# Four-layer graph network on one core: no drains between VectorE's one-hot steps, and the row chain of the first layer dealt out anew

## The chip, the core and the metric

One core of a Trainium2 chip runs the whole program in one launch. The metric is the device time of that launch in microseconds; of a kernel several runs are shown, and their median is compared. A page of the profile and a trace come from one further, profiled execution.

## What is computed

6250 nodes of 128 features, 206,250 directed edges sorted by destination. Each of four layers normalizes the rows, applies relu, sums messages over the edges and adds a result to the residual stream. The change touches the first layer alone:

```python
h = jnp.maximum(_layernorm(x, axis=-1), 0.0)
msg = edge_val[:, None] * h[edge_src]
neighbor = segment_sum(msg, edge_dst, num_segments=6250)
out = neighbor @ W1.T + b1 + (h * neighbor) @ W2.T + b2
x = x + leaky_relu(out, negative_slope=0.2)
h = jnp.maximum(_layernorm(x, axis=-1), 0.0)      # rows for layer 2
```

Layers 2 to 4 (two aggregations over the same edges, a graph norm, a gated update) reuse a table of edge counts that the first layer's stage leaves in DRAM.

## The kernel before

**Sorting and tables** (to about 130 us): edges are laid into groups; four tables (key, source low part, high and low part of the edge weight) end up in `carry`.

**The counting stage** (about 130 to 1190 us) is where the change lies. The nodes are cut into 49 blocks of 128; a *half* h handles the edges into block h. A half has 8 *duos* (`DUOS`), a duo has 2 *supergroups* (16 per half, `SGS`). The engines split the work, each in its own hand-written order, joined by semaphores:

- **VectorE** (`half_onehots`, L1691) makes the one-hot tiles of a duo in a ring of four slots (`RING`). `make_onehots` waits until TensorE has used the slot (`weight_ready`), then writes source and cell one-hots (L1634, L1635). `weigh_onehots` multiplies the cell one-hots by the two weight parts (L1639, L1640) and raises `onehots`. In step j it makes duo j and weighs duo j-1, so that no instruction follows directly on one it depends on; then come pieces of the *row chain* of older blocks, and a `dve.drain()` (L1721) closes the step.
- **TensorE** (`half`, L833) takes a duo when `onehots` says so: per supergroup 4 matmuls for counts (L800) and 8 for weights (L806) into PSUM. After every fourth supergroup comes a part of `weigh` (L817): 24 or 26 float32 instructions that multiply last half's weights with the normalized rows, so that a whole weighted sum of one block takes 98 of them. A transpose (`row_T`, L826) and two matmuls (`lin1`, L830, L831) of the row chain stand between.
- **ScalarE** (`take_half`, L1195) copies counts (L1176) and weights (L1182) of each supergroup out of PSUM; TensorE may be two supergroups ahead in counts and four in weights. It also scales the block's sum (`take_sum`, L1193, in the first supergroup of a half) and takes the square root of the row chain (`row_std`, L1186).
- **SyncE** (`half`, L494) stores the counts, loads and stores rows.

**The row chain** of block g: `prod1` (sum times h), `lin1`, `add_bias1`, `leaky`, `add_x`, `row_stats`, `row_mean`, `row_var`, the square root on ScalarE, `row_rstd`, `row_norm`, `row_relu` (two instructions), `row_rest`. Before, it is spread over the steps of halves g+2 (`prod1` in step 6), g+3 (steps 0 to 5, and 7) and g+4 (steps 0 to 2).

Halves 0 to 4 are written out as straight code on VectorE; from half 5 on two halves make one turn of a loop (`dve.Fori`), in which addresses and semaphore values come from registers. After the loop the rest of the row chain of the last blocks runs alone (the *tail*), then the edge counts are read back for the next layer (L887, L917).

```python
for j in range(DUOS):
    make_onehots(h * DUOS + j, j % RING)
    if not (first and j == 0):
        weigh_onehots(h * DUOS + j - 1, (j - 1) % RING)
    ...
    dve.drain()
```

Of the kernel before, what the change touches and what calls it, by code (L numbers as in the profile page):

```python
# [42 lines left out]
RING = 4  # L43
# [38 lines left out]
def build_gnn(nc, A, out):  # L82
    with ExitStack() as ctx:
# [264 lines left out]
        def _(sp):  # L348
# [141 lines left out]
            def count_sorted():  # L490
# [94 lines left out]
            branch(sp, order, edges_any(3), load_pieces(3))  # L585
# [140 lines left out]
        def _(pe):  # L726
# [381 lines left out]
        def _(act):  # L1108
# [86 lines left out]
            def take_half(h, par, i, summed=True, normed=True):  # L1195
                for s in range(SGS):
# [3 lines left out]
                    if s == 9 and normed:  # L1200
                        row_std(h - 3)

            def count_sorted():
# [8 lines left out]
                with act.Fori(1, NHALF // 2) as i:  # L1212
                    take_half(i * 2 + 1, 1, i)
                    take_half(i * 2 + 2, 0, i + 1)
                take_sum(NB - 2, 1)
                row_std(NB - 3)
# [143 lines left out]
        def _(dve):  # L1360
# [330 lines left out]
            def half_onehots(h, par, summed=True, last=True, oldest=True, first=False):  # L1691

                for j in range(DUOS):
                    make_onehots(h * DUOS + j, j % RING)
                    if not (first and j == 0):
                        weigh_onehots(h * DUOS + j - 1, (j - 1) % RING)
                    if oldest:
                        if j == 0:
                            row_norm(par)
                        if j == 1:  # L1700
                            row_relu(h - 4, par)
                        if j == 2:
                            row_rest(h - 4, par)
                    if last:
                        if j == 0:
                            add_bias1(h - 3)
                        if j == 1:
                            leaky()
                        if j == 2:
                            add_x(h - 3, 1 - par)  # L1710
                        if j == 3:
                            row_stats(1 - par)
                        if j == 4:
                            row_mean()
                        if j == 5:
                            row_var()
                        if j == 7:
                            row_rstd(h - 3)
# [17 lines left out]
            def row_planes(g, par):  # L1736
# [5 lines left out]

            def row_end(g, par):
                row_rstd(g)
                dve.drain()
                row_planes(g, par)
# [16 lines left out]
            def count_sorted():  # L1763
# [3 lines left out]
                half_onehots(0, 0, False, False, False, True)  # L1767
                half_onehots(1, 1, False, False, False)
                half_onehots(2, 0, True, False, False)
                half_onehots(3, 1, True, True, False)  # L1770
                half_onehots(4, 0)
                with dve.Fori(2, NHALF // 2) as i:
                    half_onehots(i * 2 + 1, 1)
                    half_onehots(i * 2 + 2, 0)
                weigh_onehots(NDUO - 1, RING - 1)

                dve.drain()
                for j in range(3):
# [4 lines left out]
                row_planes(NB - 4, 1)  # L1783
                row_sum(NB - 3, 0)
                prod1(NB - 2, 1)
                row_end(NB - 3, 0)
                row_sum(NB - 2, 1)
                prod1(NB - 1, 0)
                row_end(NB - 2, 1)
                row_sum(NB - 1, 0)  # L1790
# [257 lines left out]
```

## Time and profile before

| | |
|---|---|
| median of 3 runs | 2363.23 us (2360.51 to 2366.76) |
| profiled execution | 2367.89 us, its span 2366.2 us |
| PE / PEld / DVE / ACT busy | 2041.8 / 1810.6 / 1538.2 / 1229.5 us |
| counting stage: PE, DVE, ACT busy of 1036.40 us (154.40 to 1190.80) | 1009.72, 904.39, 631.35 us |
| largest groups | L1176 398.6, L817 577.0, L806 417.9, L1182 407.8, L1634 271.5, L1639, L1640, L1635 219.5 us each |

Busy times are unions of an engine's instructions; matmuls are pipelined, so a busy PE isn't PE at its peak. An instruction's duration reaches past the start of the next one where the two overlap, so a step is measured from start to start. A wait on "issue" is idle time for which the trace shows no instruction that ended it.

### The profile page before, as it was taken

How to read it: one execution, taken by the hardware profiler on the slowest of the kernel's cores; microseconds unless marked ns; L12 is line 12 of the kernel's file. 1: busy time of each engine (PE TensorE's matmuls, PEld its weight loads, DVE VectorE, ACT ScalarE, POOL GpSimd, SP SyncE). 2: the span in 40 equal slices, each digit the busy share in tenths (PEclk: the TensorE clock that was granted, in tenths of full speed). 3: DMA queues.
4: the chain of work that ended last, by engine and by line, in shares of the span. 5: the costliest groups of instructions: out<-in, count | busy, mean ns of one | idle time of the engine just before them, and what ended most of it. 6: DMA issues, size and time to landing. Idle time of an engine off the chain costs nothing.

```text
span 2366.2 us, 63380 instructions
## 1 busy us (share of the span) xinstructions
PE 2041.8 (86%) x22497; PEld 1810.6 (77%) x22542; DVE 1538.2 (65%) x3147; ACT 1229.5 (52%) x3115; POOL 136.3 (6%) x120
## 2 busy tenths in 40 slices
PE   1269999999999999999989999999986239999897
PEld 1169999999999999999976666668886238888444
DVE  8588888888888888888855565657855850000133
ACT  4856666666666666666636676678865200000232
POOL 5500000000000000000000000000002410000000
PEclk7579999999999999999999999999998569999898
DMA  8312222122212222221243333325841459888121
GB/s 242 105 60 78 81 95 95 64 94 95 88 69 95 95 74 84 95 95 63 95 158 119 117 117 117 107 107 192 322 148 51 118 197 334 301 300 271 40 69 39
DMA packets 184330, 300.84 MB, mean 127 GB/s; under 512 B 12626, under 2 KB 135943, under 8 KB 184159
## 3 DMA queue, kind: packets, MB, share of 16 engines
q1 hardware_dynamic: 180364, 287.55, 35.0%
q0 software_dynamic: 3904, 12.50, 1.8%
q8 instruction: 35, 0.57, 0.1%
q14 instruction: 27, 0.22, 0.0%
HBM read 199.52 MB, written 100.48 MB: 127 GB/s over the span
## 4 chain that ended last, share of the span: by engine, by line
PE 40%; DVE 28%; DVEq 15%; issue 10%; ACT 2%; DMA 2%; POOL 1%; ACTq 1%; POOLq 0%; SPq 0%; PEldq 0%
PE ps L917 22%; DVEq L1721 8%; DVE edge_area L1640 7%; DVE edge_area L1635 5%; PE ps L901 5%; DVE edge_area L1639 4%; PE ps L887 3%; PE ps L1038 3%; PE ps L817 3%; DVE edge_area L1634 1%; PE ps L957 1%; DVE hT_s L1488 1%; DVEq L1634 1%; POOL edge_area L643 1%; PE ps L806 1%
## 5 line engine op out<-in xcount | busy, mean ns | idle before, releaser
L1176 ACT CAST edge_area<-ps 128x392 f16<-128x392 f32 x784 | 398.6, 508 | 422.0 <-PE ps L800 421.6
L817 PE MATMUL ps<-big,rows_area 128*128 128x128 f32 x4802 | 577.0, 277 | 0.3 <-ACT agg_s L1193 0.3
L817 PEld LDWEIGHTS ps<-big,rows_area 128*128 128x128 f32 x4802 | 551.8, 192 | 0.6 <-ACT agg_s L1193 0.6
L806 PE MATMUL ps<-edge_area 128*128 128x98 f16 x6272 | 417.9, 208 | 0.0
L1182 ACT COPY big<-ps 128x392 f32<-128x392 f32 x784 | 407.8, 520 | 1.1 <-PE ps L806 0.7
L1634 DVE TENSOR_TENSOR edge_area<-lo_pair,carry 128x1024 f16<-128x1024 f16 x392 | 271.5, 693 | 130.5 <-issue 102.8
L806 PEld LDWEIGHTS ps<-edge_area 128*128 128x128 f16 x6272 | 332.6, 98 | 0.0
L800 PE MATMUL ps<-edge_area 128*128 128x98 f16 x3136 | 276.5, 209 | 38.8 <-DVE edge_area L1640 35.5
L917 PE MATMUL ps<-big,agg 128*128 128x256 f16 (+1 forms) x2450 | 290.1, 278 | 0.0
L917 PE MATMUL ps<-big,rows_area 128*128 128x256 f16 (+1 forms) x2450 | 264.3, 272 | 25.6 <-DMA big<-edge_counts 25.6
L917 PEld LDWEIGHTS ps<-big,rows_area 128*128 128x128 f16 x2450 | 236.6, 98 | 53.5 <-DMA big<-edge_counts 25.9
L917 PEld LDWEIGHTS ps<-big,agg 128*128 128x128 f16 x2450 | 239.0, 101 | 30.6
L1248 ACT ACTIVATE edge_area<-ps,edge_area 128x896 bf16<-128x896 f32 x182 | 173.5, 1004 | 128.7 <-DVE edge_area L1822 75.4
L800 PEld LDWEIGHTS ps<-edge_area 128*128 128x128 f16 x3136 | 189.2, 98 | 61.9 <-issue 39.3
L1639 DVE TENSOR_TENSOR edge_area<-edge_area,carry 128x784 f16<-128x784 f16 x392 | 219.5, 560 | 0.2 <-issue 0.2
L1640 DVE TENSOR_TENSOR edge_area<-edge_area,carry 128x784 f16<-128x784 f16 x392 | 219.5, 560 | 0.0
L1635 DVE TENSOR_TENSOR edge_area<-cell_pair,carry 128x784 f16<-128x784 f16 x392 | 219.4, 560 | 0.0
L1266 ACT ACTIVATE edge_area<-big 128x256 f16<-128x256 f16 (+1 forms) x525 | 209.4, 404 | 15.4 <-DMA big<-edge_counts 8.2
L1843 DVE TENSOR_REDUCE out_part<-big 128x4 f32<-128x1024 f16 (+1 forms) x175 | 202.1, 1189 | 0.0
L1835 DVE TENSOR_TENSOR carry<-carry,ps 128x896 f32<-128x896 f32 x85 | 92.3, 1086 | 143.0 <-PE ps L901 143.0
L1863 DVE TENSOR_SCALAR agg<-ps 128x256 f32 (+2 forms) x25 | 10.5, 419 | 258.4 <-PE ps L917 258.4
L1327 ACT COPY hT_s<-ps 128x896 f32<-128x896 f32 x7 | 6.3, 906 | 297.2 <-PE ps L948 297.2
(235 smaller groups left out, 1854.1 us busy)
## 6 DMA issues: line engine op xcount, KB each, us to landing
big<-edge_counts SPq DMA_DIRECT2D x336, 448.0 KB, 4.6
edge_counts<-edge_area SPq DMA_DIRECT2D x49, 1568.0 KB, 5.6
hs<-node_rows POOLq DMA_DIRECT2D x14, 448.0 KB, 4.1
edge_area<-x_stream SPq DMA_DIRECT2D x14, 448.0 KB, 3.9
node_rows<-rows_area SPq DMA_DIRECT2D x1, 3136.0 KB, 13.1
agg_s<-node_rows SPq DMA_DIRECT2D x49, 64.0 KB, 4.9
agg_s<-in_x SPq DMA_DIRECT2D x49, 64.0 KB, 4.4
x_stream<-agg_s SPq DMA_DIRECT2D x49, 64.0 KB, 2.5
```

The source lines that it names most:

```text
L800: last = mm(pair_of(p_count[s % 2], c), sources_of(slot, r, c), cells_of(oh_cell, slot, r, c), start=(c == 0), stop=(c == 3), skip_group_c ...
L806: last = mm(pair_of(p_weight[s % 4], c), sources_of(slot, r, c), cells_of(oh, slot, r, c), start=(c == 0 and oh is oh_whi), stop=(c == 3 a ...
L817: last = mm(p_sum, h0[:, n, :], w32[:, par, n, :], start=(n == 0), stop=(n == NB - 1))
L917: last = mm(p_block[par][:, 0:width, :], planes1[:, sh, p, :] if l == 1 else planes[:, p, sh, :], piece[:, par, k, 0:width, j, :], start=( ...
L1176: nc.scalar.copy(store_slot[:, par, :, cols], p_count[s % 2]).then_inc(sem("count_taken"), 1)
L1182: nc.scalar.copy(w32[:, par, :, cols], p_weight[s % 4]).then_inc(sem("weight_taken"), 1)
L1266: last = nc.scalar.activation(unused[:, j, 0:width, :], piece[:, par, k, 0:width, j, :], ACT.Copy, accum_out=out_part[:, par, sh:sh + 1])
L1634: V.tensor_tensor(oh_src[:, slot], paired(lo_pair, P), lo.to_broadcast([P, 4, P, 2]), ALU.is_equal)
L1635: V.tensor_tensor(oh_cell[:, slot], paired(cell_pair, CELLS), key.to_broadcast([P, 4, CELLS, 2]), ALU.is_equal)
L1639: V.tensor_tensor(oh_whi[:, slot], oh_cell[:, slot], whi.to_broadcast([P, 4, CELLS, 2]), ALU.mult)
L1640: V.tensor_tensor(oh_wlo[:, slot], oh_cell[:, slot], wlo.to_broadcast([P, 4, CELLS, 2]), ALU.mult).then_inc(sem("onehots"), 1)
L1843: V.tensor_reduce(out_part[:, par, k * SHS:k * SHS + KD], piece[:, par, k, 0:width, 0:KD, :].rearrange("p q n d -> p n q d"), AX_XY, ALU.a ...
```

## The change

1. VectorE's steps lose their `dve.drain()`. In its place each step waits, after it has issued the one-hots of duo d, until `onehots` shows that the weights of duo d-2 are done; then the row chain's instructions follow, and `weigh_onehots` of duo d-1 closes the step (it stood right behind `make_onehots`). The very first step keeps a drain and raises `onehots` by one, and TensorE's wait goes up by one to match.
2. The row chain of block g is dealt out anew: `prod1` in step 7 of half g+2; `add_bias1`, `leaky`, `add_x`, `row_stats` in steps 4, 5, 6, 7 of half g+3; `row_mean`, `row_var` in steps 0, 1 and `row_rstd`, `row_norm`, `row_relu` in steps 5, 6, 7 of half g+4; `row_rest` in step 0 of half g+5. It ends one half later.
3. TensorE's `row_T` moves from supergroup 3 to 7, `lin1` from 11 to 15; ScalarE's square root from supergroup 9 to 3, for a block one older. SyncE stores an x row before it loads the next one.
4. In the tail, which holds one block's chain more, the instructions of two blocks alternate, with drains.

```diff
@@ SyncE
                 def half(h, b, par, older=True):
                     load_h_row(h - 1, 1 - par)
+                    store_x(h - 3, 1 - par)
                     load_x_row(h - 2, par)
-                    store_x(h - 3, 1 - par)
...
                 load_h_row(NB - 1, 0)
+                store_x(NB - 3, 0)
                 load_x_row(NB - 2, 1)
-                store_x(NB - 3, 0)
                 store_h(NB - 4, 1)
+                store_x(NB - 2, 1)
                 load_x_row(NB - 1, 0)
-                store_x(NB - 2, 1)
                 store_h(NB - 3, 0)
@@ TensorE
-                    pe.wait_ge(sem("onehots"), h * DUOS + s // 2 + 1)
+                    pe.wait_ge(sem("onehots"), h * DUOS + s // 2 + 2)
...
-                        if rows and s == 3:
+                        if rows and s == 7:
                             row_T(h - 2, par)
...
-                        if rows and s == 11:
+                        if rows and s == SGS - 1:
                             lin1(h - 2, par)
@@ ScalarE
-                    if s == 9 and normed:
-                        row_std(h - 3)
+                    if s == 3 and normed:
+                        row_std(h - 4)
@@ VectorE
                 for j in range(DUOS):
                     make_onehots(h * DUOS + j, j % RING)
-                    if not (first and j == 0):
-                        weigh_onehots(h * DUOS + j - 1, (j - 1) % RING)
+                    if first and j == 0:
+                        dve.drain()
+                        dve.sem_inc(sem("onehots"), 1)
+                        continue
+
+                    dve.wait_ge(sem("onehots"), h * DUOS + j)
+                    if written and j == 0:
+                        row_rest(h - 5, 1 - par)
                     if oldest:
                         if j == 0:
+                            dve.sem_inc(sem("passed"), 1)
+                            row_mean()
+                        if j == 1:
+                            row_var()
+                        if j == 5:
+                            row_rstd(h - 4)
+                        if j == 6:
                             row_norm(par)
-                        if j == 1:
+                        if j == 7:
                             row_relu(h - 4, par)
...
-                    if summed and j == 6:
+                    if summed and j == 7:
                         prod1(h - 2, par)
-                    dve.drain()
+                    weigh_onehots(h * DUOS + j - 1, (j - 1) % RING)
```

How the instructions stand on VectorE in the loop, the step that holds `row_var` (`TENSOR_SCALAR rstd<-mv`); ISA rows are register work, drains are not listed. Before:

```order
L1632 ISA
L1634 ISA [waits weight_ready]
L1634 TENSOR_TENSOR edge_area<-lo_pair,carry 128x1024
L1635 ISA
L1635 TENSOR_TENSOR edge_area<-cell_pair,carry 128x784
L1639 ISA
L1639 TENSOR_TENSOR edge_area<-edge_area,carry 128x784
L1640 ISA
L1640 TENSOR_TENSOR edge_area<-edge_area,carry 128x784
L1667 TENSOR_SCALAR rstd<-mv 128x1
```

The same step of the change (its lines are numbered six higher):

```order
L1638 ISA
L1640 ISA [waits weight_ready]
L1640 TENSOR_TENSOR edge_area<-lo_pair,carry 128x1024
L1641 ISA
L1641 TENSOR_TENSOR edge_area<-cell_pair,carry 128x784
L1673 TENSOR_SCALAR rstd<-mv 128x1 [waits onehots]
L1645 ISA
L1645 TENSOR_TENSOR edge_area<-edge_area,carry 128x784
L1646 ISA
L1646 TENSOR_TENSOR edge_area<-edge_area,carry 128x784
```

The row instruction now stands between making and weighing, and carries the wait on `onehots`; the number of instructions is the same.

The last step of a half in the change, VectorE, with the most row instructions of all steps:

```order
L1687 ISA [waits onehots]
L1688 TENSOR_SCALAR hT_s<-hT_s 128x128 [waits h1_out]
L1690 ISA
L1690 TENSOR_SCALAR agg<-hT_s 128x128
L1667 BN_STATS stats<-agg_s 128x6
L1650 REGISTER_ALU
L1653 TENSOR_TENSOR agg_s<-ps,agg_s 128x128 [waits hT1,sum_taken]
L1645 ISA
L1645 TENSOR_TENSOR edge_area<-edge_area,carry 128x784
```

Before, these four instructions stood in steps 1, 3 and 6; now all are ahead of the weighing of duo 6, and the last of them waits for TensorE's transpose (`hT1`).

## Rows read from the trace of the kernel before

**Rows 1.** The page, part 4: the chain that ended last, by engine and line.
```profile
PE 40%; DVE 28%; DVEq 15%; issue 10%; ACT 2%; DMA 2%; POOL 1%; ACTq 1%; POOLq 0%; SPq 0%; PEldq 0%
PE ps L917 22%; DVEq L1721 8%; DVE edge_area L1640 7%; DVE edge_area L1635 5%; PE ps L901 5%; DVE edge_area L1639 4%; PE ps L887 3%; PE ps L1038 3%; PE ps L817 3%; DVE edge_area L1634 1%; PE ps L957 1%; DVE hT_s L1488 1%; DVEq L1634 1%; POOL edge_area L643 1%; PE ps L806 1%
```
**Rows 2.** Waits, 130 to 1190 us: who waited for whom, us, times, longest.
```profile
DVE edge_area L1634 <- issue: 102.8, 284, 3.3
PE ps L800 <- DVE edge_area L1640: 35.5, 71, 7.1
```
**Rows 3.** Timeline, ScalarE, the copy of a block's sum: start, duration.
```profile
194.62 0.38 ACT L1193 ACTIVATE agg_s<-ps,w_unit 128x128 f32<-128x128 f32 x1
215.69 0.38 ACT L1193 ACTIVATE agg_s<-ps,w_unit 128x128 f32<-128x128 f32 x1
...
605.50 0.38 ACT L1193 ACTIVATE agg_s<-ps,w_unit 128x128 f32<-128x128 f32 x1
...
1170.31 0.38 ACT L1193 ACTIVATE agg_s<-ps,w_unit 128x128 f32<-128x128 f32 x1
```
**Rows 4.** Timeline, VectorE, straight code, a step without row instructions.
```profile
155.51 0.69 DVE L1634 TENSOR_TENSOR edge_area<-lo_pair,carry 128x1024 f16<-128x1024 f16 x1
156.12 0.56 DVE L1635 TENSOR_TENSOR edge_area<-cell_pair,carry 128x784 f16<-128x784 f16 x1
...
157.08 0.56 DVE L1640 TENSOR_TENSOR edge_area<-edge_area,carry 128x784 f16<-128x784 f16 x1
157.73 0.69 DVE L1634 TENSOR_TENSOR edge_area<-lo_pair,carry 128x1024 f16<-128x1024 f16 x1
```
**Rows 5.** Timeline, VectorE, straight code, end of the step with `row_var`.
```profile
221.42 0.56 DVE L1640 TENSOR_TENSOR edge_area<-edge_area,carry 128x784 f16<-128x784 f16 x1
221.90 0.15 DVE L1667 TENSOR_SCALAR rstd<-mv 128x1 f32<-128x1 f32 x1
222.14 0.69 DVE L1634 TENSOR_TENSOR edge_area<-lo_pair,carry 128x1024 f16<-128x1024 f16 x1
```
**Rows 6.** Timeline, VectorE, in the loop, end of the same step.
```profile
613.04 0.56 DVE L1640 TENSOR_TENSOR edge_area<-edge_area,carry 128x784 f16<-128x784 f16 x1
613.52 0.15 DVE L1667 TENSOR_SCALAR rstd<-mv 128x1 f32<-128x1 f32 x1
613.99 0.69 DVE L1634 TENSOR_TENSOR edge_area<-lo_pair,carry 128x1024 f16<-128x1024 f16 x1 [0.32 <-issue]
```
**Rows 7.** Windows: two halves at the loop's start, and one half in its middle.
```profile
217.10:259.20 42.10, 41.85 (x592) 41.16 (x590) 36.62 (x86) 26.27 (x69) 0.00 (x0) 1.00 0.25 89
600.10:621.96 21.86, 21.49 (x306) 20.94 (x303) 18.95 (x45) 13.59 (x36) 0.00 (x0) 1.00 0.24 85
```
**Rows 8.** Timeline, VectorE, in the loop, two row instructions in a row.
```profile
605.53 0.28 DVE L1688 SCALAR_TENSOR_TENSOR agg<-hT_s,agg 128x128 f32 x1
605.73 0.28 DVE L1658 TENSOR_TENSOR agg_s<-agg_s,hT_s 128x128 f32<-128x128 f32 x1
```
**Rows 9.** The chain in order of time, half 3: start, us, what.
```profile
194.88 0.51 ACT edge_area L1176
195.43 0.35 PE ps L800 x4
...
196.29 2.68 PE ps L817 x24
```
**Rows 10.** The chain in order of time, where it passes from VectorE to TensorE.
```profile
153.27 0.36 PE ps L800 x4
```
**Rows 11.** Timeline, the tail of the stage and the start of the next.
```profile
1202.92 0.37 ACT L1193 ACTIVATE agg_s<-ps,w_unit 128x128 f32<-128x128 f32 x1 [11.65 <-PE ps L817]
...
1204.37 4.28 PE L867 MATMUL ps<-carry,pick_row 128*25 128x128 f16 x75
...
1214.15 1.65 PE L887 MATMUL ps<-ident,big 128*128 128x128 f16 x14 [5.50 <-issue]
```
**Rows 12.** Timeline, VectorE, a wait for ScalarE's square root.
```profile
227.06 0.16 DVE L1671 RECIPROCAL rstd<-rstd 128x1 f32<-128x1 f32 x1 [0.38 <-ACT rstd L1186]
```

More of the change, by code:

```diff
@@ L584, in _, with summed_any @@
             stage(2, x_dram)
-            branch(sp, order, edges_any(3), load_pieces(3))
+            def summed_any():
+                sp.wait_ge(sem("agg_done"), 3)
+            branch(sp, order, both(edges_any(3), summed_any), load_pieces(3))
             sp.dma_start(hs[:], rows_of(rows_dram, 0)).then_inc(sem("h_in4"), 16)
@@ L1211, in count_sorted @@
                 take_half(2, 0, 1, True, False)
-                with act.Fori(1, NHALF // 2) as i:
+                take_half(3, 1, 1, True, False)
+                take_half(4, 0, 2)
+                with act.Fori(2, NHALF // 2) as i:
                     take_half(i * 2 + 1, 1, i)
@@ L1215, in count_sorted @@
                 take_sum(NB - 2, 1)
+                row_std(NB - 4)
                 row_std(NB - 3)
@@ L1689, in row_rest, with half_onehots @@
                                        op1=ALU.subtract).then_inc(sem("planes_ready1"), 1)
-            def half_onehots(h, par, summed=True, last=True, oldest=True, first=False):
+            def half_onehots(h, par, first=False, summed=True, last=True, oldest=True, written=True):
                 for j in range(DUOS):
                     make_onehots(h * DUOS + j, j % RING)
-                    if not (first and j == 0):
-                        weigh_onehots(h * DUOS + j - 1, (j - 1) % RING)
+                    if first and j == 0:
[5 more added lines that the diff above has]
+                        row_rest(h - 5, 1 - par)
@@ L1697, in half_onehots @@
                     if oldest:
                         if j == 0:
+                            dve.sem_inc(sem("passed"), 1)
[5 more added lines that the diff above has]
+                        if j == 6:
                             row_norm(par)
-                        if j == 1:
+                        if j == 7:
                             row_relu(h - 4, par)
-                        if j == 2:
-                            row_rest(h - 4, par)
@@ L1704, in half_onehots @@
                     if last:
-                        if j == 0:
+                        if j == 4:
                             add_bias1(h - 3)
-                        if j == 1:
+                        if j == 5:
                             leaky()
-                        if j == 2:
+                        if j == 6:
                             add_x(h - 3, 1 - par)
-                        if j == 3:
+                        if j == 7:
                             row_stats(1 - par)
-                        if j == 4:
-                            row_mean()
@@ L1715, in half_onehots @@
[L1715 to L1718, printed above, removed]
-                    if summed and j == 6:
+                    if summed and j == 7:
                         prod1(h - 2, par)
-                    dve.drain()
+                    weigh_onehots(h * DUOS + j - 1, (j - 1) % RING)
             def row_sum(g, par):
@@ L1734, in row_sum, with row_end @@
                 row_var()
-            def row_planes(g, par):
+            def row_end(g, par):
+                row_rstd(g)
+                dve.drain()
                 row_norm(par)
@@ L1741, in row_planes @@
                 row_rest(g, par)
[L1743 to L1746, printed above, removed]
             def rows_any():
@@ L1766, in count_sorted @@
                 dve.sem_inc(sem("mix_added"), 1)
[L1767 to L1771, printed above, removed]
+                half_onehots(0, 0, True, False, False, False, False)
+                half_onehots(1, 1, False, False, False, False, False)
+                half_onehots(2, 0, False, True, False, False, False)
+                half_onehots(3, 1, False, True, True, False, False)
+                half_onehots(4, 0, False, True, True, True, False)
                 with dve.Fori(2, NHALF // 2) as i:
@@ L1774, in count_sorted @@
                     half_onehots(i * 2 + 2, 0)
+                dve.drain()
                 weigh_onehots(NDUO - 1, RING - 1)
+                row_rest(NB - 5, 0)
+                add_bias1(NB - 3)
+                row_mean()
                 dve.drain()
+                leaky()
+                row_var()
                 for j in range(3):
@@ L1782, in count_sorted @@
                 V.memset(pick_row[:, DEG_BLOCKS - 1:DEG_BLOCKS], 1.0).then_inc(sem("bad_known"), 1)
-                row_planes(NB - 4, 1)
-                row_sum(NB - 3, 0)
-                prod1(NB - 2, 1)
-                row_end(NB - 3, 0)
-                row_sum(NB - 2, 1)
-                prod1(NB - 1, 0)
-                row_end(NB - 2, 1)
-                row_sum(NB - 1, 0)
+                add_x(NB - 3, 0)
+                row_rstd(NB - 4)
+                dve.drain()
+                row_stats(0)
+                row_norm(1)
+                dve.drain()
+                prod1(NB - 2, 1)
+                row_relu(NB - 4, 1)
+                row_mean()
+                dve.drain()
+                row_var()
+                row_rest(NB - 4, 1)
+                add_bias1(NB - 2)
+                dve.drain()
+                leaky()
+                row_rstd(NB - 3)
+                dve.drain()
+                add_x(NB - 2, 1)
+                row_norm(0)
+                dve.drain()
+                row_stats(1)
+                row_relu(NB - 3, 0)
+                dve.drain()
+                row_mean()
+                row_rest(NB - 3, 0)
+                dve.drain()
+                row_var()
+                prod1(NB - 1, 0)
+                dve.drain()
+                row_rstd(NB - 2)
+                add_bias1(NB - 1)
+                dve.drain()
+                leaky()
+                row_norm(1)
+                dve.drain()
+                add_x(NB - 1, 0)
+                row_relu(NB - 2, 1)
+                dve.drain()
+                row_stats(0)
+                row_rest(NB - 2, 1)
+                dve.drain()
+                row_mean()
+                dve.drain()
+                row_var()
                 row_end(NB - 1, 0)
```

## The prediction

> **What bounds the kernel now.** I read the chain that ended last first, because busy shares alone mislead here: the table has TensorE at 97% of the counting stage, yet the chain gives VectorE 28% of the span and VectorE's queue (DVEq) another 15%, and the one line L1721, the drain of `half_onehots`, has 8% by itself [rows 1]. 43% of a span of 2366.2 us is about 1017 us, which is nearly the counting stage: VectorE sets its pace. The waits say how: VectorE stood idle 284 times before L1634, the first instruction of a step, for 102.8 us in all with nothing but "issue" behind it, and TensorE waited 71 times for L1640 [rows 2].
>
> Next, the pace. ScalarE copies a block's sum once per half, always at the same place, so the distance of two copies is a half's period. It is 21.07 us from 194.62 to 215.69; from 215.69 to 1170.31 there are 44 halves in 954.62 us, 21.70 us each [rows 3]. The reader is to see that the same work runs at two paces. The early pace belongs to halves that VectorE had prepared in straight code, the late one to the loop. At the fast pace the chain runs through ScalarE's copy and TensorE [rows 9], and TensorE is busy 41.85 of 42.10 us [rows 7]: that is TensorE's own limit, with the same row chain in it. The difference, 0.63 us per half, is what VectorE costs today, and all that can be had from relieving it.
>
> **The cost of a drain.** Four one-hot instructions start 0.61, 0.48, 0.48 and, if nothing were between, 0.48 us apart: 2.05 us. Behind L1640 the next step starts 0.65 us later instead of 0.48 [rows 4], so in straight code a drain costs 0.17 us. With one short row instruction in the step, the next step follows 0.24 us after that instruction in straight code [rows 5] but 0.47 us in the loop [rows 6]. In the loop the register rows that compute addresses stand ahead of L1634, and behind a drain they can't be done while VectorE works. Between L1634 and L1640 there are register rows in the loop too, and the one-hots there start no farther apart than in straight code. So without the drain I expect both parts to go, the flush and the register work.
>
> **VectorE's need without drains.** One half in the loop has 45 instructions, 18.95 us busy of 21.86 [rows 7]. The busy time counts the last 0.08 us of L1640 (0.56 less 0.48), which overlaps with a successor once there is no drain: 8 of these take it to 18.3 us. Counted the other way: 8 steps of 2.05 are 16.4 us; 13 row instructions of some 0.15 to 0.34 us follow each other closer than they last, 0.20 for one of 0.28 [rows 8], some 1.9 us; together 18.3 us. TensorE's pace is 21.07. VectorE is left with 2.7 us per half, a third of a microsecond per step, before it sets the pace again.
>
> **What takes its place.** Each step now waits for `onehots` of duo d-2. Those weights were issued before the two one-hots of duo d: L1640 ends 0.08 us after its successor would start, and the instruction that carries the wait stands 1.09 us behind that start (0.61 and 0.48). I cost the new wait at nothing; the cover is the pair of one-hots. Its bounds: nothing, and at most what the drain cost.
>
> **The moved row chain.** No instruction is added in a half; on TensorE one transpose and four lin1 instructions move to other gaps of the same kind, so its pace stays. Who waits for whom: `prod1` in step 7 waits for the transpose behind supergroup 7; step 7 can only begin when TensorE has left duo 3, which is supergroup 7, so the transpose is finished while the one-hots of step 7 are made. `add_bias1` in step 4 needs `lin1` of the half before, and step 4 begins only when TensorE is through duo 0 of the next half, which is behind that lin1. `row_rstd` in step 5 needs ScalarE's root, which now stands behind the copies of supergroup 3, the very one that releases step 5: a wait like the 0.38 us of [rows 12] is likely every half. It is covered by the 2.7 us; without that cover it would cost 0.4 us times 45 halves, 17 us. Behind it in VectorE's queue is the weighing of duo 4, which TensorE needs only after it has worked through two duos and one part of `weigh` (2.7 us, [rows 9]). SyncE's queue: the store of x now waits for step 6 and h for step 7 instead of 2 and 1, and the counts of the half are stored behind them; both steps lie before TensorE ends the half, so nothing is late.
>
> **The sum**, against the profiled execution (2367.89 us):
> - The loop. 954.62 us less 44 times 21.07 (927.08) is 27.5 us; the 45th half, up to the tail, gives another 0.6. Minus 28.1 us.
> - The start. Until 153.27 us TensorE waits for VectorE duo by duo, without `weigh` [rows 10]: nine steps, 0.17 us each. Minus 1.5 us.
> - The tail. From the last sum copy on it is a chain of single instructions, and the next stage begins 5.50 us after TensorE's last count matmul with "issue" behind it [rows 11], which doesn't change. The last block's chain starts sooner behind `lin1`, but its instructions share their steps with another block's: three more of 0.2 to 0.3 us against 0.5 saved. The x row of the last block is loaded later, perhaps just late. Plus 0.3 us, between minus 1 and plus 3.
>
> Together minus 29.3 us: 2338.6 us for that execution. The median of the runs shown is 4.66 us below it, so 2333.9 us.
>
> **A rule that speaks against it.** The rows say that L1640 starts 0.48 us after an instruction that lasts 0.56, and 0.65 us after it where a drain stands between [rows 4]: the explicit drain costs something that instructions without one do not pay. The Trainium skill ("VectorE: DVE Perf Modes", section "The DRAIN you can't avoid") says that the pipe is flushed after every VectorE instruction whatever one does, that chaining copies without semaphores saved nothing, and that one should count instructions, not waits. By that rule the time would stay at 2363. The trace disagrees as far as it goes.
>
> **Rivals.**
> *No gain: the wait costs what the drain did.* If the wait for `onehots` keeps VectorE from preparing what follows, each step still loses the 0.42 us it loses today ((21.70 less 18.35) by 8), and the time stays at 2363. For it: the wait is a true dependency on VectorE's own work. Against it: it is met a good microsecond before it is asked for. The section of the skill named above supports this outcome by another road. Chance 0.06.
> *A partial gain: VectorE is free, but something in the new order holds TensorE.* The wait for the root [rows 12], or the crowded step 7, shows through at 0.25 to 0.45 us per half: 45 times that is 11 to 20 us given back, 2345 to 2354. Against it: the 2.7 us, and the ring of four. Chance 0.10.
> *More than TensorE's early pace.* In the first part of a half the sum copy delays the next count copy on ScalarE, which starts 0.26 us after it (194.88 after 194.62) and which TensorE then waits for [rows 3, 9]. If the new order removes that, up to 45 times 0.26, 12 us more: 2322. For it: little, the copy stands where it stood. Chance 0.05.
> *Slower: the wait stops VectorE a second time in each step.* Each step already stops at `weight_ready` when TensorE sets the pace. If the wait for `onehots` stopped it too, and each stop cost the 0.32 us that an issue behind a drain costs in the loop [rows 6], a step would lose 0.64 us: 8 times 2.69, 1.9 for the row instructions and 0.2 for the loop's turn make 23.6 us, plus 1.9 per half, 45 times, plus 86: 2449. It decides from a loss of 0.42 us per step, today's. Against it: the same microsecond. Chance 0.03.
>
> **How the numbers follow.** The forecast, VectorE off the path and TensorE at 21.07 us per half, has 0.76. What a measurement of this kernel can tell from no change is about 0.3%, 7 us. Faster by more: 0.76, 0.10 and 0.05, together 0.91. Within 0.3%: 0.06. Slower: 0.03. A period off by 0.15 us either way moves the time by 7 us and the tail by 3, so the range runs from 2325 to 2346; it leaves out both cases without a gain and the outer parts of the two others, some 0.18.
>
> **What would show it right.** In the profile after: the drain's line is gone from the chain and VectorE with it, from half 1 on, with L817, L806 and ScalarE's copies of TensorE's results in its place; sum copies are 21.07 us apart all through; VectorE is idle before its first one-hot and TensorE's weight matmuls end that idle time, not "issue"; inside a step starts are 0.48 us apart across the wait. The new root wait of some 0.4 us shows on VectorE and moves nothing. It would be wrong if copies stood 21.3 us or more apart (then look at what TensorE's counts wait for), or if idle time on "issue" before the first one-hot stayed near 0.3 us with TensorE waiting behind it.

## The result, and the profile after

The changed kernel takes 2328.22 us, the median of 4 runs (2326.54 to 2336.32), against 2363.56 us (2360.51 to 2366.76, 4 runs) for the kernel before: a ratio of 0.9862, with a 95% interval of 0.9836 to 0.9887. The profiled execution took 2327.56 us, its span is 2325.9 us.

The page of the changed kernel, part 4, the chain that ended last, to be laid beside [rows 1]:

```profile
PE 77%; DVE 9%; issue 4%; ACT 4%; DVEq 2%; DMA 2%; POOL 1%; ACTq 1%; POOLq 0%; SPq 0%; PEldq 0%
PE ps L820 23%; PE ps L920 22%; PE ps L809 10%; PE ps L803 6%; PE ps L904 5%; PE ps L890 3%; PE ps L1041 3%; PE ps L960 1%; DVE hT_s L1494 1%; POOL edge_area L646 1%; ACT edge_area L1179 1%; DMA hs<-node_rows 1%; ACT edge_area L1132 1%; PE ps L968 1%; DVE carry L1544 1%
```

VectorE's 28% and its queue's 15% have shrunk to 9% and 2%, and no one-hot line and no drain is left among the lines. L820 (L817 before), TensorE's matmuls of the sum, has gone from 3% to 23%. The chain does not say that TensorE does more; it says that the path through the counting stage now runs over TensorE.

The waits of the changed kernel, 130 to 1170 us (who waited for whom: us, times, longest), to be laid beside [rows 2]:

```profile
DVE edge_area L1640 <- PE ps L809: 125.5, 143, 1.5
...
PEld ps L803 <- ACT edge_area L1179: 12.9, 47, 0.3
PE ps L803 <- DVE edge_area L1646: 11.9, 8, 7.2
```

The idle time of VectorE before a step is still there, and as long. What has changed is who ends it. Before it was "issue", 284 times and 102.8 us, and TensorE's weight matmuls only in the rest of the steps, as this line of the kernel before shows:

```profile
DVE edge_area L1634 <- PE ps L806: 24.5, 72, 1.0
```

That makes 127.3 us. Now it is TensorE's weight matmuls, 143 times and 125.5 us: VectorE has finished and waits for a free slot. TensorE's waits for VectorE have fallen from 71 to 8. There is one short wait per half of TensorE's weight loads (PEld) for ScalarE's count copy, 0.3 us, which an experiment below goes after.

Timeline of the changed kernel, ScalarE, the copy of a block's sum (start, duration, line, what), to be laid beside [rows 3]; the last row is the tail's:

```profile
193.41 0.38 ACT L1196 ACTIVATE agg_s<-ps,w_unit 128x128 f32<-128x128 f32 x1
214.47 0.38 ACT L1196 ACTIVATE agg_s<-ps,w_unit 128x128 f32<-128x128 f32 x1
...
614.64 0.38 ACT L1196 ACTIVATE agg_s<-ps,w_unit 128x128 f32<-128x128 f32 x1
635.71 0.38 ACT L1196 ACTIVATE agg_s<-ps,w_unit 128x128 f32<-128x128 f32 x1
...
1141.21 0.38 ACT L1196 ACTIVATE agg_s<-ps,w_unit 128x128 f32<-128x128 f32 x1
1160.88 0.37 ACT L1196 ACTIVATE agg_s<-ps,w_unit 128x128 f32<-128x128 f32 x1 [1.85 <-PE ps L820]
1173.44 0.37 ACT L1196 ACTIVATE agg_s<-ps,w_unit 128x128 f32<-128x128 f32 x1 [6.17 <-PE ps L820]
```

There is one pace now: 21.06 us early, 21.07 in the middle, and from 214.47 to 1141.21 there are 44 halves of 21.06. Against the 954.62 us of the same 44 halves before, this subtraction of two rows gives 27.9 of the 29.0 us that the counting stage lost.

Timeline of the changed kernel, VectorE in the loop, the step with `row_var` (L1673), to be laid beside [rows 6]:

```profile
606.63 0.69 DVE L1640 TENSOR_TENSOR edge_area<-lo_pair,carry 128x1024 f16<-128x1024 f16 x1
607.24 0.57 DVE L1641 TENSOR_TENSOR edge_area<-cell_pair,carry 128x784 f16<-128x784 f16 x1
607.71 0.16 DVE L1673 TENSOR_SCALAR rstd<-mv 128x1 f32<-128x1 f32 x1
607.77 0.57 DVE L1645 TENSOR_TENSOR edge_area<-edge_area,carry 128x784 f16<-128x784 f16 x1
608.25 0.57 DVE L1646 TENSOR_TENSOR edge_area<-edge_area,carry 128x784 f16<-128x784 f16 x1
```

L1673 carries the new wait on `onehots`. It starts 0.47 us after L1641, as any successor does, and the next one-hot follows 0.06 us later. The wait is not to be seen, and in its new place the short row instruction costs next to nothing either.

### The profile page after: what moved, and what is told of

Same layout as the page of the kernel before. It is cut to its first block, busy times and chain, and to the rows that moved or that the text cites. A ratio compares the mean times of both kernels' runs of the same rounds, so it can differ in the third digit from the quotient of the medians.

```text
span 2325.9 us, 63176 instructions
## 1 busy us (share of the span) xinstructions
PE 2026.4 (87%) x22542; PEld 1803.5 (78%) x22542; DVE 1512.0 (65%) x3147; ACT 1228.5 (53%) x3115; POOL 136.5 (6%) x120
## 4 chain that ended last, share of the span: by engine, by line
PE 77%; DVE 9%; issue 4%; ACT 4%; DVEq 2%; DMA 2%; POOL 1%; ACTq 1%; POOLq 0%; SPq 0%; PEldq 0%
PE ps L820 23%; PE ps L920 22%; PE ps L809 10%; PE ps L803 6%; PE ps L904 5%; PE ps L890 3%; PE ps L1041 3%; PE ps L960 1%; DVE hT_s L1494 1%; POOL edge_area L646 1%; ACT edge_area L1179 1%; DMA hs<-node_rows 1%; ACT edge_area L1132 1%; PE ps L968 1%; DVE carry L1544 1%
## 5 line engine op out<-in xcount | busy, mean ns | idle before, releaser
L1179 ACT CAST edge_area<-ps 128x392 f16<-128x392 f32 x784 | 407.1, 519 | 393.7 <-PE ps L803 393.7
L820 PE MATMUL ps<-big,rows_area 128*128 128x128 f32 x4802 | 576.9, 277 | 0.0
L820 PEld LDWEIGHTS ps<-big,rows_area 128*128 128x128 f32 x4802 | 551.9, 192 | 0.0
L1185 ACT COPY big<-ps 128x392 f32<-128x392 f32 x784 | 416.8, 532 | 0.4 <-PE ps L809 0.3
L1640 DVE TENSOR_TENSOR edge_area<-lo_pair,carry 128x1024 f16<-128x1024 f16 x392 | 270.1, 689 | 129.0 <-PE ps L809 125.5
L1641 DVE TENSOR_TENSOR edge_area<-cell_pair,carry 128x784 f16<-128x784 f16 x392 | 220.0, 561 | 0.0
L1892 DVE TENSOR_REDUCE out_part<-big 128x4 f32<-128x1024 f16 (+1 forms) x175 | 202.1, 1190 | 0.4
```

The source lines that it names most:

```text
L820: last = mm(p_sum, h0[:, n, :], w32[:, par, n, :], start=(n == 0), stop=(n == NB - 1))
L1179: nc.scalar.copy(store_slot[:, par, :, cols], p_count[s % 2]).then_inc(sem("count_taken"), 1)
L1185: nc.scalar.copy(w32[:, par, :, cols], p_weight[s % 4]).then_inc(sem("weight_taken"), 1)
L1640: V.tensor_tensor(oh_src[:, slot], paired(lo_pair, P), lo.to_broadcast([P, 4, P, 2]), ALU.is_equal)
L1641: V.tensor_tensor(oh_cell[:, slot], paired(cell_pair, CELLS), key.to_broadcast([P, 4, CELLS, 2]), ALU.is_equal)
L1892: V.tensor_reduce(out_part[:, par, k * SHS:k * SHS + KD], piece[:, par, k, 0:width, 0:KD, :].rearrange("p q n d -> p n q d"), AX_XY, ALU.a ...
```

## Experiments

### The same two kernels again

No edit. These two ask what part of the result is the change and what part is one execution's.

The changed kernel:

> The changed kernel once more. In the profiled execution 40.3 us of span went, of which 29.5 us by the copy of the last block's sum (1202.92 to 1173.44) and 29.0 us by the next stage's first flips (1214.15 to 1185.13); the other 11 us went later, where the change touches nothing, and there TensorE's granted clock differed (0.66 against 0.89 in the first 30 us of the last stage). Theory A: that part is where the clock happens to rise, and differs from one execution to the next by some 3 to 8 us; the counting stage repeats within 0.5 us. Theory B: it belongs to the changed program, and repeats to within 1 us.

The kernel before:

> The kernel before once more, for the same question. Theory A: the stages behind the counting stage take some us more or less than in the first profile (1152 us from the first flips at 1214.15 to the end at 2366.2). Theory B: they take the same to within 1 us.

Measured: the changed kernel 2328.48 us (2327.85 to 2336.38, 4 runs) against 2363.39 us (2358.49 to 2367.53, 15 runs), ratio 0.9852 (0.9837 to 0.9867). One further run of the kernel before, the profiled one, took 2366.07 us. In the second profile of the changed kernel halves are 21.07 us and the last sum copy is at 1173.86 us, 0.4 us from the first one's. But from the first matmuls of the next stage (L890) to the end it took 1149.2 us, where the first profile has 1140.8. The kernel before took 1152.05 and 1149.4 us for the same part. So the end of the counting stage repeats to half a microsecond in the changed kernel and to 0.9 us in the kernel before (1215.02 against 1214.15), and what follows differs by 8.4 us between two executions of one program.

Windows of 30 us in the last stage, from the transposes with which it begins (L948, L951 after; in the second profile of the changed kernel these start at 2171.05, 1 us inside the window); columns: stretch, length, busy us (count) of PE, PEld, DVE, ACT, POOL, granted clock of TensorE, DMA share, GB/s. The kernel before:

```profile
2201.75:2231.75 30.00, 26.93 (x57) 12.22 (x58) 2.24 (x2) 8.17 (x9) 2.07 (x1) 0.68 0.10 31
```

The changed kernel, first profile:

```profile
2168.94:2198.94 30.00, 26.84 (x78) 13.29 (x79) 5.51 (x5) 10.88 (x11) 2.07 (x1) 0.90 0.11 31
```

The changed kernel, second profile:

```profile
2170.00:2200.00 30.00, 25.88 (x56) 11.55 (x57) 2.11 (x2) 7.92 (x8) 2.07 (x1) 0.72 0.10 31
```

The engine is as busy in all three, but it does 78 matmuls at a clock of 0.90, and 57 and 56 at 0.68 and 0.72. The same program stands in the second and the third. Of the profiled executions' difference of 40.3 us of span, 29.0 lie in the counting stage.

The twelve profiles of this case settle the larger part of the other 11.3 us. From those transposes to the end, the last stage takes one of two lengths: 156.95 to 157.27 us, at a granted clock of 0.94 or 0.95, in six profiles, and 163.65 to 164.48 us, at 0.88 to 0.89, in the six others. The changed kernel has one of each (156.96 and 163.65). Both profiles of the kernel before have the long one (164.45 and 164.48), and so has the next experiment; the two kernels below that differ from each other by the places of the root and `lin1` alone have one each (156.95 and 164.44). So 7.5 of the 11.3 us come from a difference that two executions of one program show too (6.7 us there). What decides between the two lengths no run here shows.

### The drains back, the new deal kept

```diff
                     weigh_onehots(h * DUOS + j - 1, (j - 1) % RING)
+                    dve.drain()
```

> The changed kernel with a drain at the end of each step again; the new deal of the row chain, the waits and the other engines' places stay. If the drains were what cost (my theory), VectorE sets the pace again: 8 steps of 2.05, 1.9 for row instructions, 8 stops of 0.39, 0.2 for the loop's turn, 21.6 us per half instead of 21.06, the time about 2350 to 2356. Rival, that the new deal brought the gain: 21.06 per half and 2328.

Measured: 2364.73 us (2359.39 to 2368.28, 10 runs), ratio 1.0003 (0.9993 to 1.0014): the kernel before, within the noise. Halves in the loop are 21.61 and 21.86 us by turns, 21.74 in the mean, against 21.53 and 21.92, 21.72 in the mean, in the kernel before; the early ones, in straight code, keep 21.07. I had expected a remainder of gain, 2350 to 2356 us; there is none. The pace was wrong by some 0.13 us per half, 6 us in 45 halves; the other part of the miss lies behind the counting stage, which here ends at 1213.85 us, 0.3 us before that of the kernel before.

Timeline of this kernel, VectorE in the loop, the end of a step without row instructions:

```profile
603.73 0.56 DVE L1646 TENSOR_TENSOR edge_area<-edge_area,carry 128x784 f16<-128x784 f16 x1
604.61 0.69 DVE L1640 TENSOR_TENSOR edge_area<-lo_pair,carry 128x1024 f16<-128x1024 f16 x1 [0.32 <-issue]
```

Starts 0.88 us apart where the changed kernel has 0.47 (606.16 to 606.63): 0.40 us for one drain in the loop, against 0.17 in straight code [rows 4]. How these 0.40 us divide between the flush and the register rows behind it no run separates. Its waits, 130 to 1200 us:

```profile
DVE edge_area L1640 <- issue: 99.4, 264, 3.3
```

The row of before is back, nearly in full [rows 2]. The new deal without the removal brings nothing to the pace.

### The drains out, the old deal kept

The row chain's instructions stay in the steps where they stood before, and ScalarE's root and TensorE's `lin1` at their supergroups; only the form of a step is the new one. A drain ahead of the very last weighing is added as in the change.

```diff
-                    pe.wait_ge(sem("onehots"), h * DUOS + s // 2 + 1)
+                    pe.wait_ge(sem("onehots"), h * DUOS + s // 2 + 2)
...
                     make_onehots(h * DUOS + j, j % RING)
-                    if not (first and j == 0):
-                        weigh_onehots(h * DUOS + j - 1, (j - 1) % RING)
+                    if first and j == 0:
+                        dve.drain()
+                        dve.sem_inc(sem("onehots"), 1)
+                        continue
+                    dve.wait_ge(sem("onehots"), h * DUOS + j)
+                    dve.sem_inc(sem("passed"), 1)
...
-                    dve.drain()
+                    weigh_onehots(h * DUOS + j - 1, (j - 1) % RING)
...
+                dve.drain()
                 weigh_onehots(NDUO - 1, RING - 1)
```

> The kernel before with the drains alone taken out: VectorE's steps in the new form (make, wait, row instructions, weigh), but every row instruction in its old step, and TensorE, ScalarE and SyncE as before. My theory of the new deal: in step 7 row_rstd waits for a root that ScalarE takes only behind supergroup 9, while the step is released by supergroup 7; in step 0 add_bias1 waits for the lin1 behind supergroup 11, while the step is released by supergroup 9; so the weights of duo 7 come about 0.8 us late for TensorE in each half, the period is about 21.9 us (21.4 to 22.3) and the time about 2366 (2345 to 2385): without the new deal nothing is gained. Rival, that the drains are all: 21.06 and 2328.

Measured: 2352.23 us (2349.12 to 2356.75, 10 runs), ratio 0.9952 (0.9939 to 0.9966) to 2362.89 us. The half is 21.48 us all through. A loss beside the full change shows as foretold, half as large: 0.42 us per half over the 21.06 of the changed kernel. Taking out the drains alone, then, gains 11 us, and with the new deal 35; I had expected nothing (2366 us). Timeline of this kernel, VectorE, the two row instructions that wait:

```profile
612.89 0.16 DVE L1671 RECIPROCAL rstd<-rstd 128x1 f32<-128x1 f32 x1 [2.06 <-ACT rstd L1186]
...
616.38 0.29 DVE L1651 TENSOR_TENSOR hT_s<-ps,gain 128x128 f32<-128x128 f32 x1 [0.99 <-PE ps L831]
```

Of the same kernel, TensorE:

```profile
617.76 0.36 PE L800 MATMUL ps<-edge_area 128*128 128x98 f16 x4 [0.30 <-DVE edge_area L1640]
```

VectorE stops twice, for the root in step 7 and for `lin1` in step 0 of the next half, and then TensorE waits 0.30 us for the one-hots behind. By time the root is the larger wait (2.06 us). Which of the two is the cause can't be read from here, since the first takes time from the second.

### Which wait holds the old deal

Three kernels, each the one above with one or two places changed. They ran on another chip, on which the kernel before takes 2380.45 us (2373.0 to 2382.68, 13 runs) and the counting stage of these three begins some 15 us later; so ratios and periods are compared.

The root alone, two supergroups earlier:

```diff
-                    if s == 9 and normed:
+                    if s == 7 and normed:
                         row_std(h - 3)
```

> The kernel without drains and with the old deal of the row chain had 21.48 us per half, 0.41 above TensorE's 21.07; VectorE waited 2.06 us per half for ScalarE's root and 0.99 us, one step later, for TensorE's lin1. Here the root alone is taken two supergroups earlier. Theory L (the late lin1 is the last to let VectorE go): VectorE comes earlier and waits some 3 us for lin1 instead; the period stays at 21.48 us and the time at 2352 us. Theory R (the late root is what holds): the period falls to 21.07 us and the time to 2335 us.

`lin1` alone, four supergroups earlier:

```diff
-                        if rows and s == 11:
+                        if rows and s == 7:
                             lin1(h - 2, par)
```

> Here lin1 alone stands at supergroup 7 instead of 11, the root at 9 as before. Theory L: the 0.99 us wait for lin1 goes, VectorE is some 1 us earlier at the step TensorE waited for, and the period falls to 21.07 us, 2335 us. Theory R: the wait for the root stays at 2 us and the period at 21.48 us, 2352 us.

Both of these edits:

> Both moved: root and lin1 at supergroup 7. Theories L and R: the period is 21.07 us and the time 2335 us, like the change, with the row chain one half shorter than there. If neither wait is the cause (the places of the row instructions in the steps are), it stays above 21.3 us and 2345 us.

Measured: the root alone 0.9962 (0.9948 to 0.9976), halves of 21.48 us. `lin1` alone 0.9873 (0.9846 to 0.9900), halves of 21.06. Both 0.9866 (0.9838 to 0.9893), halves of 21.05. Theory L holds in each. With the root earlier, VectorE doesn't wait for it any more, but stands at `lin1` for 2.79 us instead of 0.99, and TensorE waits as before. Timeline, root alone, VectorE and then TensorE:

```profile
632.47 0.29 DVE L1651 TENSOR_TENSOR hT_s<-ps,gain 128x128 f32<-128x128 f32 x1 [2.79 <-PE ps L831]
```

```profile
633.85 0.36 PE L800 MATMUL ps<-edge_area 128*128 128x98 f16 x4 [0.30 <-DVE edge_area L1640]
```

Timeline, `lin1` alone, VectorE:

```profile
619.99 0.16 DVE L1671 RECIPROCAL rstd<-rstd 128x1 f32<-128x1 f32 x1 [2.74 <-ACT rstd L1186]
...
622.41 0.28 DVE L1651 TENSOR_TENSOR hT_s<-ps,gain 128x128 f32<-128x128 f32 x1
```

This kernel waits 2.74 us per half for the root, more than any other here, and its counting stage is as fast as the change's: 1054.65 us from the first one-hot (144.84) to the next stage (1199.49), against 1054.85 (130.28 to 1185.13). The wait for `lin1` is the one behind which TensorE came to stand, although it was the shorter of the two. It is also seen that the chain's extra half is not needed: what the new deal does for the time, moving `lin1` alone does too.

### The sum's copy ahead of the half

The rival "more than TensorE's early pace", tried on the changed kernel: ScalarE takes the block's sum before the first supergroup of a half instead of behind it.

```diff
             def take_half(h, par, i, summed=True, normed=True):
+                if summed:
+                    take_sum(h - 2, par)
                 for s in range(SGS):
                     take_supergroup(h, par, i, s)
-                    if s == 0 and summed:
-                        take_sum(h - 2, par)
```

> The changed kernel with ScalarE's copy of a block's sum moved ahead of the half's first supergroup, where ScalarE waits 2.5 us for TensorE anyway (2.48 us idle before L1179 at 613.88). If TensorE's pace of 21.06 holds a stall behind that copy (the 0.29 us wait at 615.45), a half takes 20.8 us, and the time falls by 46 times 0.26, 12 us, to 2316. Rival: the copy waits for the end of the weighing, and TensorE waits elsewhere instead (for the sum, or for the first counts): no change, or slower by as much.

Measured: 2316.17 us (2314.53 to 2324.75, 5 runs), ratio 0.9808 (0.9790 to 0.9827). Timeline of this kernel, ScalarE:

```profile
607.80 0.37 ACT L1196 ACTIVATE agg_s<-ps,w_unit 128x128 f32<-128x128 f32 x1 [1.85 <-PE ps L820]
628.62 0.37 ACT L1196 ACTIVATE agg_s<-ps,w_unit 128x128 f32<-128x128 f32 x1 [1.85 <-PE ps L820]
649.44 0.37 ACT L1196 ACTIVATE agg_s<-ps,w_unit 128x128 f32<-128x128 f32 x1 [1.85 <-PE ps L820]
```

20.82 us per half, 0.24 less than the change, and the wait of TensorE's weight loads for L1179 (12.9 us, 47 times in the changed kernel) is gone from the waits. The copy now falls into time in which ScalarE waits for TensorE anyway, and no longer stands ahead of a count copy that TensorE needs. This version is 12 us faster than the change and the fastest of all that were run.

### How much room VectorE has

An extra instruction of known length in each step of the changed kernel, a memset of a spare tile of 256 or 512 float32 per partition. In the traces it takes 0.27 and 0.48 us. The edit is shown with 512.

```diff
+        spare = sb("spare", [P, 512])
...
                         prod1(h - 2, par)
+                    V.memset(spare[:], 0.0)
                     weigh_onehots(h * DUOS + j - 1, (j - 1) % RING)
```

With 256:

> The changed kernel with one more VectorE instruction in each step, a memset of a spare tile of 128x256 float32 (by the 0.81 us of a 128x896 one some 0.25 us each, 2 us per half; it computes nothing). If VectorE has 2.7 us to spare per half, nothing changes: 21.06 per half, 2328. Rival, that waits inside the steps eat the spare time: 21.3 or more per half, 2340 or more.

With 512:

> The same with 128x512 (some 0.47 us each, 3.8 us per half). VectorE's need is then 18.3 and 3.8, and 0.2 for the loop's turn where it shows, 22.1 to 22.3 us, 1.1 us over TensorE's pace: 46 times 1.1, 50 us, the time about 2378 (2370 to 2385). If it stays near 2328, VectorE needs less than I think.

Measured with 256: 2335.47 us (2333.18 to 2340.06, 4 runs), ratio 0.9886 (0.9858 to 0.9913), halves of 21.07 as without it. Of VectorE's idle time 48.7 us are left of 125.5. In the profile the next stage begins 1.2 to 1.6 us later than in the two profiles of the change, and the 1.8 us by which the early sum copies are later account for it (195.17 against 193.41); the loop adds nothing. The median is 7 us above the change's; the rest of that is not in the counting stage but behind it, where two executions of the changed kernel differ by as much; its cause is not shown.

Measured with 512: 2380.66 us (2379.41 to 2384.74, 4 runs), ratio 1.0078 (1.0051 to 1.0104), halves of 22.03 us. The windows of one half of this kernel (columns as above):

```profile
1000.00:1022.03 22.03, 21.06 (x300) 20.67 (x298) 22.03 (x56) 13.29 (x35) 0.00 (x0) 1.00 0.23 86
```

Its waits, 130 to 1200 us (its lines are one higher):

```profile
PE ps L804 <- DVE edge_area L1647: 51.6, 53, 7.9
```

VectorE is busy without a gap, and TensorE waits for it about once per half. Three steps in a row start here, the first with `row_var` in it, the second without any row instruction:

```profile
608.23 1.00 DVE L1641 TENSOR_TENSOR edge_area<-lo_pair,carry 128x1024 f16<-128x1024 f16 x1
...
610.80 1.00 DVE L1641 TENSOR_TENSOR edge_area<-lo_pair,carry 128x1024 f16<-128x1024 f16 x1
...
613.31 1.00 DVE L1641 TENSOR_TENSOR edge_area<-lo_pair,carry 128x1024 f16<-128x1024 f16 x1
```

The second takes 2.51 us, against some 2.04 for four one-hots: the memset adds 0.47, about its own duration. (The first is 0.06 us longer.) Eight of 0.48 are 3.8 us, and 22.03 less 3.8 leaves 18.2 us, as an estimate, for VectorE's own work in a half.

## Why the prediction was right

The forecast was 2333.9 us in a range of 2325 to 2346; the time is 2328.2. Point by point:

**VectorE set the pace, through its drains.** Shown. With drains and new deal the loss is all there (2364.73 us), at 0.40 us a drain in the loop; the text had 0.42 us per step. That the register rows behind the drain are what makes it dearer in the loop was argued in the text and fits, but no run took them apart.

**TensorE at 21.07 us takes over.** Shown; 21.06. But the text calls this "TensorE's own limit", and that it is not: with the sum's copy earlier a half takes 20.82 us, so 0.24 us of it is time in which TensorE stands for ScalarE. The number held because the change leaves that wait alone. From row to row:

| term | predicted | measured | from |
|---|---|---|---|
| 44 halves of the loop | -27.5 | -27.9 | 954.62 less 926.74 |
| the 45th half | -0.6 | -0.8 | 20.50 less 19.67 |
| the start | -1.5 | -1.2 | 215.69 less 214.47 |
| the tail | +0.3 | +0.9 | 12.56 less 12.11, and 11.69 less 11.23 up to the next stage |
| sum | -29.3 | -29.0 | 1214.15 less 1185.13 |

The 45th half and the tail's distance of copies belong to the new deal and not to the drains: with the drains back they are 19.67 and 12.56 us as in the change, and with the old deal and no drains 20.10 and 12.12. The text had counted the former with the loop's gain.

The first VectorE instruction of the stage started 0.4 us later in this execution than in the one before (130.28 against 129.89), so the start in itself gained 1.6. The tail, where three more row instructions were counted against shorter waits, lost 0.6 more than I had it; its 0.9 us lie half in the last sum's distance (0.45) and half in what follows it (0.46).

**The new wait costs nothing.** Shown by the step with `row_var` above. It is asked for long after it is met.

**VectorE's need, 18.3 us, and 2.7 us of cover.** Borne out: 18.2 by the larger memset. Of the two memsets the one of 0.27 us was hidden and the one of 0.48 us broke through, on either side of the third of a microsecond per step that the text gives as room.

**The wait for the root.** Wrong. I expected it at 0.4 us on VectorE in each half, by [rows 12]; in the loop of the changed kernel there is none. The root is done at 617.44 us and VectorE asks for it at 618.26. I had placed the wait by the order alone, as if the slot's release started step 5. It doesn't: VectorE waits for TensorE ahead of step 4 (1.52 us, until 614.94), and step 5 follows behind step 4 at 617.18 without a wait. When it comes to the root, 1.08 us later, that has been done for 0.8 us. It would have been harmless: with `lin1` moved alone, 2.74 us per half are waited for the root at no cost.

**What the prediction left out.** It priced the moved row chain at nothing, as something that does no harm. It was needed: taken alone, the removal of the drains brings 11 us, not 35, since with the old places VectorE stands at `lin1` and TensorE's next counts then wait 0.30 us for the one-hots behind. I worked out who waits for whom in the new order only, and never asked what the old order would do once the drains were gone. The waits of before did not show it (L1651 waited 3.6 us in all there): a VectorE that is late finds every result ready.

**The rival with 2322 us** was given 0.05, because the copy of the sum stands where it stood. That was right for this change: the 0.3 us wait is there 47 times. The price was right too; the experiment that removes it has 0.24 us per half and 12 us in all.

**The 5.7 us between forecast and median** are not in the counting stage, where the terms fit to 0.3 us in the profiled execution. They lie behind it: that part took 1140.8 and 1149.2 us in two executions of the changed kernel and 1152.05 and 1149.4 us of the kernel before. The medians differ by 35 us in both comparisons, 6 more than the stage gives. A good part is likely the last stage with its two lengths, 7 us apart: of the eight runs of the changed kernel six took 2326.54 to 2328.87 us and two 2336.3, while those of the kernel before spread over 2358.49 to 2367.53 us, so one median lies at the lower end of its range and the other in the middle. The longest runs of the two kernels differ by 30.4 and 31.2 us, close to what the stage gives. Whether the changed kernel has the short last stage more often as a rule stays open; the forecast had nothing for it, and that the median came within 5.7 us owes something to luck.

**The rule that spoke against it.** As the prediction reads the Trainium skill ("VectorE: DVE Perf Modes", section "The DRAIN you can't avoid"), the time would have stayed where it was. That reading goes further than the section: it speaks of a flush behind each instruction and of semaphores, not of what an explicit drain costs, and adds that a next instruction that is not held starts earlier. (The advice to count instructions stands in the same page's section "Rules for kernel authors".) For an explicit drain the measurement decides: with the drain the starts of two one-hots are 0.88 us apart in the loop, without it 0.47, at durations of 0.56, and the removal of some 390 of them, with the order that lets TensorE profit from it, takes 29 us from the counting stage. On the skill's flush after each single instruction these rows say only that a start may come 0.09 us before the end that the profile gives its predecessor.

## What to carry to other kernels

When the waits show an engine idle before its own next instruction with only "issue" as the releaser, look for a drain: here one cost 0.17 us in straight code and 0.40 us in a loop with addresses from registers. A wait on the engine's own semaphore, raised a step earlier, took its place and cost nothing that could be measured. Before such an engine is sped up, list what it will then ask for, and move those producers earlier. Which wait matters was told here not by its length but by what another engine stood for next, and only moving one producer at a time showed it. Then read what the new bound waits for: here a copy of 0.38 us on a third engine, one place too late, was worth another 12 us.

## What the hardware showed unexpectedly

- A drain costs 0.17 us in straight code and 0.40 us in the loop, with no row instruction involved; I had seen the dearer price only where one stood ahead of it. At the loop's turn the idle time on "issue" is 0.73 us with a drain; in the changed kernel no step of the loop has "issue" ahead of its first one-hot.
- A row instruction of 0.16 us between two one-hots moves the next one-hot by 0.06 us (607.71 to 607.77), less than half of its duration.
- The granted clock at one place of the last stage was 0.68, 0.72 and 0.90 in three executions, two of them of the same program. In twelve profiles of ten kernels the last stage took either some 157 us (clock 0.94 or 0.95) or some 164 us (0.88 to 0.89), and nothing between. Of the 8.4 us between the two profiles of the changed kernel 6.7 lie there.
- The start of the counting stage lay 15 us later on one chip than on the two others, in all three profiles that were taken there (first one-hot at 144.84 to 146.15 us instead of some 130).
